# Softplus in two scans: from one activation to absolute value, exponential, logarithm and a sum

## The chip, the cores and the metric

The kernel runs on one core of one Trainium2 chip. The metric is the device time of one execution in microseconds (us). Three runs of the kernel before took 1286.11, 1288.93 and 1290.60 us; the median is 1288.93 us.

## The reference, cut to what matters

The reference is a stack of two layers over x of shape (1, 2048, 128), float32. Each part is added to x after a layer norm of its input:

```python
# layer 0, mixer: a state-space scan with 8 heads, 16 states
dt = softplus(zxbcdt[..., -NHEADS:] + dt_bias)          # (T, 8)
h  = exp(dt_t * A) * h + dt_t * x_t[..., None] * B_t    # A = -exp(A_log)
y  = sum(h * C_t) + D * x_t ; layer norm ; gate = sigmoid(y @ W_gate.T + b_gate)
# layer 0, ffn: causal attention (16 heads of 8), then 8 experts with exact gelu, top 2 gated
# layer 1, mixer: a scan with 256 channels and 16 states
xc    = silu(conv(x @ in_proj_w ...))
delta_s, B, u = split(xc @ x_proj_w + x_proj_b)
delta = softplus(delta_s @ dt_proj_w + dt_proj_b)       # (T, 256)
h     = exp(delta * A) * h + delta * B * u              # A = -1 ... -16
y     = (h.sum(-1) + u * D) * silu(z)
# layer 1, ffn: gated net with ternary weights, silu and gelu
```

The two uses of softplus are the subject: softplus(v) = log(1 + exp(v)), which equals max(v, 0) + log(1 + exp(-|v|)).

## The kernel before, in words

All engines run hand-written programs; every wait is a semaphore in `S`, and each engine works through its own list in order. Tokens are treated in NB = 4 blocks of BLK = 512, each of TPB = 4 chunks of 128.

**Mixer of layer 0.** Steps g = 0 ... 21, one per chunk (`chunk_act`, `chunk_front_dve` and so on), and between them pieces of the next block ("front", b+1) and of the last ("end", b-1), placed by `mixer_parts`: in step g with c = g % 4 the front part c of block g // 4 + 1 is done after the chunk's own work. `front_act` part 2 (L559 to L567) computes dt (Softplus, L563) and then two Silu into `sz` (L567); `front_late_dve` part 2 multiplies `sz` into `skip` (L713); in the next step `front_early_dve` part 3 makes dtA (L688) and its running sum cs (L694). `chunk_act` (L615) makes 8 exponentials of cs per chunk, `front_act` part 3 more exponentials (L574, L577) and four Silu (L581, L583). `end_act` part 3 is a Tanh (L641). At the very start ScalarE makes `a_neg` (L2424), and VectorE's first layer norm (L352) is queued behind the operation that reads it (L2452). The weights and the x of block 0 arrive under `in_x`.

**Attention** runs from about 200 to 720 us and is not touched. **Experts** (`moe_act`, `moe_pe`, `moe_dve`) go through 32 units k: ScalarE does Gelu on four tiles (L1630), TensorE the products up (L386 to L388) of unit k and down (L1620) of unit k-1, VectorE the gating (L1638). Block 0 of the second scan's front is put between the last units by `MF_PE`, `MF_ACT`, `MF_DVE`: dt products (L1896) and Softplus (L1963) at k = 29, u at 30 (L1884, L1948), du at 31 (L1998). The four banks of unit k's up product are freed one by one by unit k-1's Gelu.

**Scan of layer 1.** 64 steps (block b, state n). In each, ScalarE makes decay = exp(-(n+1) delta) of 128x1024 into psum (L2015) once step k-2 is scanned, and copies the last column of step k-2 (L2084); GpSimd makes drive = du * B of 128x1024 (L2055), up to five steps ahead; VectorE scans twice over 512 (L2077); TensorE adds the states up in psum (L2006). The front of block b+1 is spread over the 16 steps of block b by the tables `FRONT_PE`, `FRONT_ACT`, `FRONT_DVE`; an entry (n, part) is done on that engine after the work of step n:

```python
FRONT_PE  = [..., (8, "db"), (10, "dt"), (12, "u")]
FRONT_ACT = [..., (7, "xc"), (7, "gate"), (8, "db"), (11, "dt"), (12, "u")]
FRONT_DVE = [(-9, "stats"), (4, "conv0"), (5, "conv1"), (13, "du")]
```

"xc" and "gate" are Silu (L1939, L1942). "dt" on TensorE is L1896, on ScalarE the Softplus L1963 out of two psum banks. "u" on TensorE is L1884, whose two results go into the same two banks, so it waits for `c_dt_read`, which L1963 raises; on ScalarE "u" (L1948) waits for `c_u_filled`. "du" on VectorE is (u + bias) * delta (L1998); GpSimd's first drive of the next block waits for it (`delta_ready`). TensorE's own queue puts the sum of state k-3 ahead of the front parts of step k. The loads of ScalarE's function tables are not written in the source; the build puts one ahead of an activation whose function is not in the set that is loaded, and the profile shows it under that activation's line.

## Time and profile before

| | |
|---|---|
| median of 3 runs | 1288.93 us |
| the profiled execution | 1292.51 us, span 1290.7 us, mean granted clock 0.964 |
| PE (matmul) busy | 1147.6 us, 89% |
| VectorE (DVE) busy | 874.0 us, 68% |
| ScalarE (ACT) busy | 746.6 us, 58%, 1116 instructions |
| GpSimd (POOL) busy | 313.3 us, 24% |

The stages by the trace: layer 0 mixer 0 to about 200 us, attention to 720, experts to 946, scan to 1150, the last net to the end. Busy shares are means over stages that are bound by different engines, so each stage is read by itself. Times of rows are us from the span's start.

### The profile page before, as it was taken

What the parts mean: (1) busy time and instruction counts of PE and PEld (TensorE: products, weight loads), DVE (VectorE), ACT (ScalarE), POOL (GpSimd) and SP (SyncE); (2) the same over time, 40 slices, a digit from 0 to 9 for tenths busy, and PEclk for the clock granted to TensorE, in tenths of its full rate; (3) what the DMA queues carried; (4) which work ended last, traced back from release to release, by engine and by line L of the source; (5) the groups of instructions that cost most, each with busy time, mean ns of one, the idle gap of its engine ahead of it and who ended that gap; (6) DMA issues with size and microseconds to landing.
All of it is one profiled execution on the core that took longest, in us unless ns stands there. A gap on an engine that the chain in (4) does not pass through costs nothing.

```text
span 1290.7 us, 15518 instructions
## 1 busy us (share of the span) xinstructions
PE 1147.6 (89%) x5584; PEld 573.3 (44%) x5584; DVE 874.0 (68%) x1660; ACT 746.6 (58%) x1116; POOL 313.3 (24%) x260
## 2 busy tenths in 40 slices
PE   5799777888999999999999999999968889779998
PEld 2455443433333333333322565655523334347776
DVE  4788658958888888878843443444369999964443
ACT  5677532455665565646688544445658676435554
POOL 4323321210010000000011300000079788830000
PEclk9889889999999999989999999999989899889999
DMA  5210553344000000000000312211132223100000
GB/s 163 82 56 29 164 122 82 91 107 92 2 2 2 2 1 1 1 1 2 1 27 10 112 43 60 87 41 33 34 114 107 86 111 115 66 0 1 9 9 17
DMA packets 30491, 67.25 MB, mean 52 GB/s; under 512 B 3816, under 2 KB 16112, under 8 KB 28368
## 3 DMA queue, kind: packets, MB, share of 16 engines
q1 hardware_dynamic: 30416, 66.27, 17.7%
q8 instruction: 45, 0.74, 0.2%
q14 instruction: 30, 0.25, 0.1%
HBM read 57.47 MB, written 8.78 MB: 51 GB/s over the span
## 4 chain that ended last, share of the span: by engine, by line
PE 56%; DVE 15%; POOL 10%; issue 9%; ACT 9%; DMA 1%; SPq 0%; DVEq 0%; POOLq 0%; ACTq 0%
PE psum L1620 8%; PE psum L1328 8%; PE psum L1213 7%; PE psum L1282 6%; POOL drive L2055 6%; DVE mx L1225 6%; PE psum L386 5%; PE psum L388 5%; PE psum L387 5%; DVE hst L2077 2%; ACT probs L1296 2%; ACT psum L2015 1%; ACT edec L615 1%; PE psum L528 1%; PE psum L381 1%
## 5 line engine op out<-in xcount | busy, mean ns | idle before, releaser
L1225 DVE TENSOR_REDUCE mx<-psum 128x1 f32<-128x512 f32 (+3 forms) x640 | 349.2, 604 | 64.7 <-PE psum L1213 35.4
L1296 ACT ACTIVATE probs<-psum 128x1024 f32<-128x1024 f32 (+1 forms) x320 | 283.5, 936 | 171.7 <-PE psum L1282 151.3
L1213 PE MATMUL psum<-kz,qa 128*128 128x512 bf16 (+3 forms) x640 | 199.6, 354 | 22.6 <-DVE mx L1225 16.3
L1282 PE MATMUL psum<-qa,kz 128*128 128x512 bf16 (+1 forms) x640 | 174.9, 361 | 7.2 <-DMA qa<-m_rows 4.2
L1328 PE MATMUL psum<-probs,v 128*32 128x512 f32 (+3 forms) x1280 | 151.3, 544 | 1.5 <-POOL probs L1307 1.4
L1638 DVE TENSOR_TENSOR hid<-hid,gate_bc 128x1024 f32<-128x1024 f32 x64 | 79.0, 1241 | 106.7 <-ACT hid L1630 105.0
L2055 POOL TENSOR_TENSOR drive<-du,b_bc 128x1024 f32<-128x1024 f32 x64 | 148.7, 2359 | 1.4 <-issue 1.4
L2006 PE MATMUL psum<-hst,ident 128*128 128x512 f32 x256 | 122.1, 622 | 21.9 <-DVE u L2095 14.1
L1213 PEld LDWEIGHTS psum<-kz,qa 128*128 128x128 bf16 x640 | 57.1, 97 | 186.1 <-DVE mx L1225 136.9
L1630 ACT ACTIVATE hid<-psum,cols 128x512 f32<-128x512 f32 x128 | 84.7, 689 | 75.5 <-PE psum L388 75.3
L2077 DVE TENSOR_TENSOR_SCAN hst<-psum,hlast,drive 128x512 f32<-128x512 f32 x96 | 115.1, 1263 | 8.4 <-ACT psum L2015 6.4
L1307 POOL TENSOR_SCALAR_AFFINE_SELECT probs<-probs 128x512 f32<-128x512 f32 x48 | 29.4, 636 | 359.4 <-ACT probs L1296 359.4
L1620 PE MATMUL psum<-hid,ew_raw 128*128 128x512 f32 x256 | 115.4, 594 | 0.0
L2015 ACT ACTIVATE psum<-delta 128x1024 f32<-128x1024 f32 x64 | 65.6, 1025 | 55.4 <-DVE hst L2077 55.3
L2006 PEld LDWEIGHTS psum<-hst,ident 128*128 128x128 f32 x256 | 49.1, 198 | 89.8 <-issue 70.2
L1282 PEld LDWEIGHTS psum<-qa,kz 128*128 128x128 bf16 x640 | 57.3, 99 | 66.5 <-ACT probs L1296 26.9
L1620 PEld LDWEIGHTS psum<-hid,ew_raw 128*128 128x128 f32 x256 | 48.0, 189 | 51.5 <-issue 46.2
L652 DVE TENSOR_TENSOR fh_lo<-fh,fh_hi 128x512 fp32r<-128x512 f32 x48 | 32.1, 689 | 56.5 <-ACT fh_hi L2267 56.5
L386 PE MATMUL psum<-nx_hi,ew_lo 128*128 128x512 f32 x128 | 61.3, 479 | 1.0 <-POOL ew_lo L652 1.0
L386 PE MATMUL psum<-fh_hi,fw_lo 128*128 128x512 f32 x144 | 57.2, 398 | 5.4 <-DVE fh_lo L652 5.2
L388 PE MATMUL psum<-fh_hi,fw_hi 128*128 128x512 f32 x144 | 56.2, 390 | 0.0
L387 PE MATMUL psum<-fh_lo,fw_hi 128*128 128x512 f32 x144 | 56.1, 390 | 0.0
(285 smaller groups left out, 1687.8 us busy)
## 6 DMA issues: line engine op xcount, KB each, us to landing
b_bc<-b_rows SPq DMA_DIRECT2D x16, 1024.0 KB, 4.7
cs_bc<-cs_rows SPq DMA_DIRECT2D x16, 512.0 KB, 4.7
gate_bc<-gate_rows SPq DMA_DIRECT2D x32, 256.0 KB, 3.2
qk_part_rows<-qk_parts SPq DMA_DIRECT2D x48, 128.0 KB, 2.3
ew_raw<-experts_dram SPq DMA_DIRECT2D x8, 512.0 KB, 3.6
qa<-qk_part_rows SPq DMA_DIRECT2D x16, 192.0 KB, 5.3
kz<-qk_part_rows SPq DMA_DIRECT2D x16, 192.0 KB, 5.9
fw_raw<-net_dram SPq DMA_DIRECT2D x11, 256.0 KB, 2.7
```

Of the source, the lines that this page charges most:

```text
L386: pe.matmul(out, w[1], x[0], start=start, stop=False, skip_group_check=True)
L387: pe.matmul(out, w[0], x[1], start=False, stop=False, skip_group_check=True)
L388: return pe.matmul(out, w[0], x[0], start=False, stop=stop, skip_group_check=True)
L1213: ins = pe.matmul(out[:, 0:w], qa[:, b, h // 2, i * P:(i + 1) * P], key_rows(h, c)[:, 0:w], start=True, stop=not last, skip_group_check=True)
L1225: dve.tensor_reduce(mx[:, 4 * i + h % 4, c:c + 1], fill_bank("mx", k, n)[:, 0:w], AX.X, ALU.max).then_inc(S["mx_read"], 1)
L1282: ins = pe.matmul(out[:, lo:], key_rows(h, kt // TPB)[:, kt % TPB * P:(kt % TPB + 1) * P], qa[:, b, h // 2, lo:], start=True, stop=not dia ...
L1296: act.activation(probs[:, st % 2, hh, :, lo:], s_pair[n % 2][:, :, lo:], ACT.Exp, scale=SCALE).then_inc(S["p_done"], 1)
L1328: ins = pe.matmul(out[32 * hh:32 * hh + 32, own:], v9[:, at:at + 32], probs[:, st % 2, hh, j, own:], start=(kt == 0), stop=(kt == TPB * (b ...
L1620: ins = pe.matmul(bank[b][:, :], ew_raw[e % EW_SLOTS][:, FC + m, :], hid[:, n % HID_SLOTS, m, :], start=False, stop=(n == block_end[b] and ...
L2006: ins = pe.matmul(bank[j][:, :], ident[:, :], hst[:, (NS1 * b + n) % HBUF, j, :], start=(n == 0), stop=(n == NS1 - 1))
L2055: pool.tensor_tensor(drive[:, k % DRIVE_SLOTS, :, :], du[:, b % 2, :, :], rows.unsqueeze(1).broadcast_to([P, 2, BLK]), ALU.mult).then_inc( ...
L2077: ins = dve.tensor_tensor_scan(hst[:, k % HBUF, j, :], decay[k % 2][:, j, :], drive[:, k % DRIVE_SLOTS, j, :], init, ALU.mult, ALU.add)
```

## The change

Both Softplus are replaced. In the mixer, part 2 makes |v| into a new tile `dta`, max(v, 0) into dt, exp(-|v|) and log(1 + .) in `dta`, and VectorE adds the two ahead of dtA. In the second scan ScalarE makes |v| from both banks into delta, then one exponential and one logarithm over 128x1024; VectorE adds max(v, 0) from psum in a new part "dsum" at step 12 and raises `c_dt_read`. "u" moves from step 12 to 13 on TensorE and ScalarE, "du" from 13 to 14; in the experts "dsum" is at k = 30 and "u" at 31. The bias of the second softplus moves into the product: row 32 of its weights, against a row of `dB` that is 1. A table set that holds exponential and logarithm is loaded by name: once at the start, in chunks with g % 4 of 0 or 3, and after "gate". Semaphores of the gate loads and of the cs loads become one set, with counts to match. The diff, cut:

```diff
+        EXP_LN = "natural_log_exp_and_others"
 # front_act, part 2
-                act.activation(dt[b % 2][:, :], pj(DTREP), ACT.Softplus, bias=C("dt_bias")).then_inc(S["pj_act"], 1)
+                if b >= 1:
+                    act.wait_ge(S["dt_done"], b)
+                o.did(act.activation(dta[:, :], pj(DTREP), ACT.Abs, bias=C("dt_bias")))
+                act.activation(dt[b % 2][:, :], pj(DTREP), ACT.Relu, bias=C("dt_bias"))
+                o.wait()
+                o.did(act.activation(dta[:, :], dta[:, :], ACT.Exp, scale=-1.0))
+                o.wait()
+                act.activation(dta[:, :], dta[:, :], ACT.Ln, bias=one[:, 0:1]).then_inc(S["pj_act"], 1)
 # chunk_act, after its waits
+            if g % TPB in (0, TPB - 1):
+                act.preload_act_table_set(EXP_LN)
 # front_early_dve, part 3
                 dve.wait_ge(S["pj_act"], 5 * b + 3)
+                o.did(dve.tensor_tensor(dt[b % 2][:, :], dt[b % 2][:, :], dta[:, :], ALU.add))
+                o.wait()
 # experts
-        MF_PE = {..., 29: ("dt",), 30: ("u",)}
+        MF_PE = {..., 29: ("dt",), 31: ("u",)}
-                  29: ("dt",), 30: ("u",)}
-        MF_DVE = {21: ("stats",), 26: ("conv0",), 27: ("conv1",), 31: ("du",)}
+                  29: ("dt",), 31: ("u",)}
+        MF_DVE = {21: ("stats",), 26: ("conv0",), 27: ("conv1",), 30: ("dsum",), 31: ("du",)}
-        gate_in = [S[f"gate_in{n}"] for n in range(G_SLOTS)]
+        gate_in = cs_in
-            dve.wait_ge(gate_in[n % G_SLOTS], 16 * (n // G_SLOTS + 1))
+            dve.wait_ge(gate_in[n % G_SLOTS], 16 * len(range(n % G_SLOTS, G, CS_SLOTS)) + 16 * (n // G_SLOTS + 1))
 # tables of the scan (FRONT_PE; RING_FRONT changes as it does)
-        FRONT_PE = [..., (10, "dt"), (12, "u")]
-        FRONT_ACT = [..., (11, "dt"), (12, "u")]
-        FRONT_DVE = [(-9, "stats"), (4, "conv0"), (5, "conv1"), (13, "du")]
+        FRONT_PE = [..., (10, "dt"), (13, "u")]
+        FRONT_ACT = [..., (11, "dt"), (13, "u")]
+        FRONT_DVE = [(-9, "stats"), (4, "conv0"), (5, "conv1"), (12, "dsum"), (14, "du")]
 # scan_front_act, "gate"
                 act.activation(sz1[b % 2][:, :, :], sz1[b % 2][:, :, :], ACT.Silu).then_inc(S["sz_ready"], 1)
+                act.preload_act_table_set(EXP_LN)
 # scan_front_act, "dt"
                 for m in range(2):
                     act.wait_ge(S["c_dt_filled"], 2 * b + m + 1)
-                    act.activation(delta[:, b % 2, m, :], scan_bank("dt", b, m)[:, :], ACT.Softplus,
-                                   bias=C("dt1_b", m)).then_inc(S["c_dt_read"], 1)
+                    o.did(act.activation(delta[:, b % 2, m, :], scan_bank("dt", b, m)[:, :], ACT.Abs))
+                o.wait()
+                o.did(act.activation(delta[:, b % 2, :, :], delta[:, b % 2, :, :], ACT.Exp, scale=-1.0))
+                o.wait()
+                act.activation(delta[:, b % 2, :, :], delta[:, b % 2, :, :], ACT.Ln, bias=one[:, 0:1]).then_inc(S["c_ln_done"], 1)
 # scan_front_dve
+            elif part == "dsum":
+                dve.wait_ge(S["c_ln_done"], b + 1)
+                for m in range(2):
+                    dve.scalar_tensor_tensor(delta[:, b % 2, m, :], scan_bank("dt", b, m)[:, :], 0.0, delta[:, b % 2, m, :],
+                                             ALU.max, ALU.add).then_inc(S["c_dt_read"], 1)
 # ScalarE's program
             act.wait_ge(S["in_x"], 32)
+            act.preload_act_table_set(EXP_LN)
 # host_layout
+    dtw[2 * NS1] = x["L1_attn_dt_proj_b"]
-    pad = np.zeros(P - 2 * NS1, np.float32)
+    pad = np.eye(1, P - 2 * NS1, dtype=np.float32)[0]
```

## Rows read from the trace of the kernel before

**Rows 1.** The page, the chain that ended last, share of the span by engine

```profile
PE 56%; DVE 15%; POOL 10%; issue 9%; ACT 9%; DMA 1%; SPq 0%; DVEq 0%; POOLq 0%; ACTq 0%
```

**Rows 2.** Stages, 968 to 1017: us, busy of PE, PEld, DVE, ACT, POOL, clock, DMA

```profile
968.00:1017.00 49.00, 40.09 (x94) 16.56 (x92) 45.91 (x53) 35.80 (x60) 42.92 (x24) 1.00 0.30 103
```

**Rows 3.** VectorE's scans (L2077): what they waited for, us and times

```profile
  ACT psum L2015: 15.6, 9
```

**Rows 4.** Groups of ScalarE, shapes apart: count, busy us, mean ns, idle before

```profile
L1963 ACT ACTIVATE delta<-psum,cols 128x512 f32<-128x512 f32 x8 | 5.2, 685 | 2.9 <-PE psum L1896 2.9
...
L1963 ACT ACT_TABLE_LOAD x4 | 5.1, 1283 | 0.1
...
L558 ACT ACTIVATE convin<-psum 128x512 f32<-128x512 f32 x8 | 4.8, 598 | 6.6 <-PE psum L447 6.6
...
L1942 ACT ACTIVATE sz_odd<-sz_odd 128x1024 f32<-128x1024 f32 x2 | 2.1, 1056 | 0.0
```

**Rows 5.** In order of time, the start: start us, us, engine, line, what, idle

```profile
0.78 1.28 ACT L2423 ACT_TABLE_LOAD   x1 [0.78 <-PEq L2597]
3.76 0.20 ACT L2423 ACTIVATE half_gate<-cols 128x2 f32<-128x2 f32 x1 [1.69 <-DMA cols<-cols_dram]
```

**Rows 6.** VectorE at the start, in order of time

```profile
4.28 0.87 DVE L352 BATCH_NORM_STATS2 ln_st<-x_tok 128x6 f32<-128x128 f32 x4
```

**Rows 7.** ScalarE in the mixer, in order of time, block 1

```profile
47.47 1.28 ACT L563 ACT_TABLE_LOAD   x1
...
50.77 1.09 ACT L567 ACTIVATE sz<-psum 128x512 f32<-128x512 f32 x2
```

**Rows 8.** VectorE in the mixer, in order of time, blocks 1 to 3

```profile
51.49 1.28 DVE L713 TENSOR_TENSOR skip<-psum,sz 128x512 f32<-128x512 f32 x2
...
64.52 0.15 DVE L739 COPY dt_tok<-psum 128x8 f32<-128x8 f32 x1
...
86.07 1.29 DVE L713 TENSOR_TENSOR skip<-psum,sz 128x512 f32<-128x512 f32 x2 [1.99 <-ACT sz L567]
...
122.01 1.29 DVE L713 TENSOR_TENSOR skip<-psum,sz 128x512 f32<-128x512 f32 x2 [0.99 <-ACT sz L567]
```

**Rows 9.** ScalarE in the last chunk of the mixer, in order of time

```profile
166.43 2.44 ACT L615 ACTIVATE edec<-cs_bc,ncs_tok 128x128 f32<-128x128 f32 x8 [2.41 <-issue]
169.04 0.69 ACT L641 ACTIVATE sg<-psum,half_gate 128x512 f32<-128x512 f32 x1 [0.17 <-PE psum L520]
```

**Rows 10.** ScalarE in the experts: the Gelu of unit 30, in order of time

```profile
922.40 2.42 ACT L1630 ACTIVATE hid<-psum,cols 128x512 f32<-128x512 f32 x4
```

**Rows 11.** TensorE in the experts and the scan, in order of time

```profile
926.36 3.60 PE L1884 MATMUL psum<-xc,sw 128*128 128x512 f32 x8
...
981.56 3.70 PE L1884 MATMUL psum<-xc,sw 128*128 128x512 f32 x8 [1.02 <-ACT delta L1963]
```

**Rows 12.** ScalarE in the scan, steps 11 to 13 of block 0

```profile
979.52 1.28 ACT L1963 ACT_TABLE_LOAD   x1
...
983.39 1.03 ACT L2015 ACTIVATE psum<-delta 128x1024 f32<-128x1024 f32 x1
...
985.30 0.69 ACT L1948 ACTIVATE u<-psum,cols 128x512 f32<-128x512 f32 x1 [0.18 <-PE psum L1884]
```

**Rows 13.** VectorE in the scan, steps 12 to 15 of block 0

```profile
984.46 4.82 DVE L2077 TENSOR_TENSOR_SCAN hst<-psum,drive 128x512 f32<-128x512 f32 x4 [1.68 <-ACT psum L2015]
989.19 1.38 DVE L1998 SCALAR_TENSOR_TENSOR du<-psum,cols,delta 128x512 f32<-128x512 f32 x2
990.49 2.33 DVE L2077 TENSOR_TENSOR_SCAN hst<-psum,drive 128x512 f32<-128x512 f32 x2
```

**Rows 14.** GpSimd in the scan: the first drives of block 1

```profile
990.71 13.91 POOL L2055 TENSOR_TENSOR drive<-du,b_bc 128x1024 f32<-128x1024 f32 x6 [0.71 <-issue]
```

**Rows 15.** TensorE in the scan, after its two waits of 3.24 us

```profile
1004.74 8.82 PE L2006 MATMUL psum<-hst,ident 128*128 128x512 f32 x20 [3.24 <-DVE u L2095]
...
1056.89 10.52 PE L2006 MATMUL psum<-hst,ident 128*128 128x512 f32 x20 [3.24 <-DVE u L2095]
```

More of the change, by code:

```diff
@@ L51 @@
     ("fc1_b", NE * FC), ("in1_b", 4), ("conv1_w", 2 * CONV), ("conv1_b", 2), ("xu_b", 2), ("xdB_b", 1),
-    ("dt1_b", 2), ("d1", 2), ("w1_s", HC), ("w2_s", HC), ("h1_s", HC), ("h2_s", HC), ("w3_s", 1),
+    ("d1", 2), ("w1_s", HC), ("w2_s", HC), ("h1_s", HC), ("h2_s", HC), ("w3_s", 1),
     ("out1_b", 1),
@@ L164, in build @@
         convin = sb("convin", [P, 2, CONV - 1 + BLK], F32)
+        dta = sb("dta", [P, BLK], F32)
         free[0] = max(free[0], KZ[1][1])
@@ L334, in build @@
             bo_added mx_read mrow_done on_done back_copied att_done mx_filled mneg_done mrow_filled p_done p_causal
-            s_scores pv_done o_copied tok_filled back_filled att_filled rden_done gate_in0 nx2_split lg_done
-            gT_done gelu_done moe_added nx2_ready lg_filled gates_done gT_filled lgm_done ex8_done ew_split
-            gate_in1 hid_filled slot_in2 down_done hid_gated slot_in3 ew_split_hi gate_in2 moe_copied
+            s_scores pv_done o_copied tok_filled back_filled att_filled rden_done nx2_split lg_done
+            c_ln_done gT_done gelu_done moe_added nx2_ready lg_filled gates_done gT_filled lgm_done ex8_done ew_split
+            hid_filled slot_in2 down_done hid_gated slot_in3 ew_split_hi moe_copied
             moe_turned moe_pool_consts in_moe c_in_read c_u_read c_db_read c_dt_read b_saved c_mixed
@@ L585, in build @@
         cs_rows = nc.dram_tensor("cs_rows", (NB, TPB, H0, P), F32, kind="Internal").ap()
-        cs_in = [sem(f"cs_in{n}") for n in range(CS_SLOTS)]
+        cs_in = [sem(f"ring_in{n}") for n in range(CS_SLOTS)]
         def cs_save_sp(sp, b):
@@ L1810, in build @@
         LN_C = 3 * NB
-        FRONT_PE = [(0, "turn"), (1, "x"), (2, "z"), (8, "db"), (10, "dt"), (12, "u")]
-        FRONT_ACT = [(-1, "apply"), (0, "hi"), (2, "x"), (3, "z"), (3, "tap"), (7, "xc"), (7, "gate"), (8, "db"), (11, "dt"), (12, "u")]
-        FRONT_DVE = [(-9, "stats"), (4, "conv0"), (5, "conv1"), (13, "du")]
+        FRONT_PE = [(0, "turn"), (1, "x"), (2, "z"), (8, "db"), (10, "dt"), (13, "u")]
+        FRONT_ACT = [(-1, "apply"), (0, "hi"), (2, "x"), (3, "z"), (3, "tap"), (7, "xc"), (7, "gate"), (8, "db"), (11, "dt"), (13, "u")]
+        FRONT_DVE = [(-9, "stats"), (4, "conv0"), (5, "conv1"), (12, "dsum"), (14, "du")]
         FRONT_POOL = [(-2, "ln")]
-        RING_FRONT = [(0, "turn"), (1, "x"), (2, "z"), (3, "tap"), (8, "db"), (10, "dt"), (12, "u")]
+        RING_FRONT = [(0, "turn"), (1, "x"), (2, "z"), (3, "tap"), (8, "db"), (10, "dt"), (13, "u")]
         EARLIEST = -9
@@ L2581, in host_layout @@
         "xu_b": vec(xpb[2 * NS1:], 2), "xdB_b": vec(np.concatenate([xpb[0:2 * NS1], pad]), 1),
-        "dt1_b": vec(x["L1_attn_dt_proj_b"], 2),
         "d1": vec(x["L1_attn_D"], 2), "w1_s": vec(x["L1_ffn_w1_s"], HC), "w2_s": vec(x["L1_ffn_w2_s"], HC),
```

2 lines of the change are left out of this document (1 added, 1 removed).

## The prediction

> **What bounds the kernel now.** I began with the page's chain [rows 1]: it is mixed, so no single engine's saving can be read off as time, and the change has to be followed stage by stage. It touches three places: the mixer of layer 0 (0 to 200 us), the last units of the experts, and the scan. The table by stage for one block of the scan [rows 2] shows VectorE busy 45.9 of 49.0 us and GpSimd 42.9, ScalarE only 35.8. So the scan is VectorE's, with ScalarE of interest where VectorE waits for a decay: 15.6 us in nine waits over the whole scan [rows 3]. The timelines then give each place of the change.
>
> **Loads of tables.** A load takes 1.28 us [rows 4]. The load ahead of each Softplus goes (four at L563, four at L1963), and in the scan's three fronts the reload ahead of the next decay: 11. To come: one in the experts after "gate", two in the experts' dt (below), one at g = 15, where a set with the exponential is in already, and one for the Tanh behind it: 5. Six fewer in all; the other named loads stand where a load stood.
>
> **The start, +1.3.** Now the first load runs at 0.78, ahead of the wait for `cols`, and costs nothing [rows 5]. By name it stands behind the wait: `half_gate` starts 1.28 later, then `a_neg`, and VectorE's first layer norm, which starts at 4.28 right behind it [rows 6], moves by as much. Nothing covers it: all later work hangs on this norm. Bounds 0 (if the build hoists it) and 1.3; I take 1.3, since an engine's list is in order.
>
> **The mixer's four blocks, +3.5.** ScalarE: out go a load and 0.69. In come Abs and Relu (0.69 like L563, the second overlapping by 0.1), an exponential (0.60, the Copy of 128x512 in [rows 4]) and a logarithm with a bias column (0.69), with two waits for itself of some 0.05: 2.7 for 1.97, so +0.7 [rows 4, 7]. Trace and page do not differ here. VectorE: one sum of 128x512, half of `skip`'s pair, 0.65 to 0.7 [rows 8], ahead of dtA. Block 0: `sz` comes while VectorE does its convolution, the sum is open: 0.7. Block 1: `sz` ends at 51.86 and `skip` starts at 51.49 as it comes [rows 7, 8]; from there VectorE has no idle time to 64.5, so both count: 1.4. Blocks 2 and 3: VectorE waits 1.99 and 0.99 for `sz` [rows 8], so ScalarE's 0.7 counts, and the sum lies beside TensorE's gate products, on whose Tanh VectorE waits next: 0.7 each, 1.4 each without that cover. Sum 3.5, bounds 2 and 6.
>
> **Chunk 15, +1.3.** Its exponentials run from 166.43 to 168.87, and Tanh starts at 169.04 [rows 9]. A redundant load ahead of them and one ahead of Tanh put Tanh at 171.4, 2.4 later; its second half was held by TensorE to 170.76, so VectorE's product after it moves by 1.3. 
>
> **The experts, +1.3.** At k = 29 Softplus gives way to two Abs (0.60 each), an exponential of 128x1024 (1.06 [rows 4]) and a logarithm (1.15, that plus the 0.09 by which L1963 exceeds L558): 3.4 for 1.3. The set of Gelu is in and none is named there, so I count a load for the exponential and one for the logarithm, both behind the input; the load of Softplus ran while ScalarE waited for its input and cost nothing. The Gelu of unit 30, from 922.40 now [rows 10], thus starts 2.1 + 2 * 1.28 = 4.7 later, at 927.1, and frees its first bank at 927.8. TensorE now goes on at 926.5 with "u" [rows 11]; after the change the up product of unit 31 comes there and wants this bank: 1.3 idle. The load after "gate" is hidden, as the Gelu behind it ends 3 us before TensorE needs it. Bounds 0 and 3. The dsum at k = 30 has 2 us to spare before "u".
> A rule against my count: the Trainium skill, "ScalarE activation tables: per-element evaluation and per-set limits", section "Table sets in the compiler and the runtime", has loads placed by the greedy longest run, which would serve Abs, Exp and Ln with one load; the 1.3 would then be about 0. No row of before has a run that two sets could serve, so the trace is silent; it is a rival below.
>
> **The scan, three fronts, +3.35 each.** At step 11 ScalarE now spends 979.52 to 983.39 on load, Softplus, load [rows 12]: 3.87. After: 0.50 + 0.60 + 1.06 + 1.15 and two waits, 3.35. So step 12, which waits 1.68 for its decay [rows 13], starts 0.55 earlier. This is all that the six loads give here, since what replaces them is nearly as long.
> Then it is lost. TensorE's "u" needs the two banks, and only VectorE's dsum frees them, after step 12. Count from the end E of step 12. Now: step 13 (2.3), du (1.3), steps 14 and 15: step 14 starts at E + 3.6 [rows 13]. After: the first half of dsum to E + 0.74 (du's form, 1.38 for two [rows 13]), then "u" on TensorE 3.70 [rows 11], ScalarE's second read 0.69, and behind that read in ScalarE's list decay 14, 1.03 [rows 12]: step 14 starts at E + 6.2. Behind the waiting read stand decay 14 and everything later on ScalarE; VectorE has only the rest of dsum and step 13 meanwhile (to E + 3.6) and idles 2.6. Then du (1.3) follows step 14 where it went before it. So 6.2 + 1.3 - 3.6 = 3.9, less 0.55: 3.35, three times: 10.05.
> GpSimd's first drive of the next block (2.32) goes 0.14 behind du [rows 14]. Now two steps (4.5) lie between du and the step that needs this drive; after, one (2.3): late by 0.2 at most, taken as nothing.
> TensorE's clock: before "u" it now idles 1.02 [rows 11], afterwards some 4.7. Of two waits of 3.24 one left 20 products at 8.82 us, the other at 10.52 [rows 15]: between 0 and 1.7 each. I take 0.5, as a fall may also come after the products: 1.5. Scan +11.5; bounds 2 and 16.
>
> **Sum.** 1.3 + 3.5 + 1.3 + 1.3 + 11.5 = 18.9 on the profiled execution's 1292.5 (span 1290.7 and 1.8 around it): 1311.4. The median of the runs is 3.6 lower: 1307.8, say 1308. Attention and the last net are unchanged. A run-to-run difference of 0.3% (3.9 us) is about what the measurement can tell.
>
> **Rivals.**
> (1) As forecast: 1308, own range 1302 to 1315. Chance 0.60.
> (2) One load fewer in the experts (the rule above): 1308 - 1.3 = 1306.7. Chance 0.12, as nothing in the trace speaks.
> (3) The late "u" is covered. If ScalarE's read of u did not hold decay 14, each front would cost dsum's 1.3 less 0.55: 2.3 in all and no clock loss: 1298.7. Against it: the order of ScalarE's list. Chance 0.10.
> (4) Faster. The mechanism is the loads in front of the decays: in each front VectorE idles for the decay around step 12 (1.68 in block 0 [rows 13]) and after "gate", 15.6 in nine waits [rows 3]. If dsum fell into such idle time and all six loads lay on the path, 6 * 1.28 = 7.7 would come off: 1281. It decides where decay 12 comes at least 1.3 earlier than now; by my count it comes 0.55 earlier, as the new activations fill the place. Chance 0.07.
> (5) The change does not do what it says: a set loaded by name is not kept by the build's placement, and each Exp and each Ln brings its own load: in the scan 2 * 1.28 more per front, in the mixer 1.28 per block: + 7.7 + 5.1: 1321. Chance 0.06.
> (6) Gains and losses cancel, within 0.3%: "u" covered and most of the mixer's terms too. Chance 0.05.
>
> **How the numbers follow.** The time is that of (1). Range 1297 to 1316: it holds (1) with its bounds, (2) and (3), and leaves out (4), (5), (6), 0.18. Faster: (4), 0.07. Within 0.3%: (6), 0.05. Slower: the rest, 0.88.
>
> **What would show it.** Right: six fewer table loads, none at L563 or at the scan's "dt"; the first norm at about 5.6; in the experts Gelu of unit 30 near 927 + 6; per front of the scan, VectorE idle 2 to 3 us after step 13 for a decay, TensorE's "u" 3 us later than now and behind dsum, ScalarE waiting for u. Scan 10 to 13 us longer. Wrong: step 14 starting right behind step 13, decays 12 coming more than 1 us earlier, or the mixer's end moved by less than 2 us.

## The result, and the profile after

The changed kernel takes 1320.49 us (median of 4 runs, 1319.09 to 1322.39), against 1288.78 us before: ratio 1.0249, interval 1.0226 to 1.0271, so 32 us slower. The direction was forecast and the size was not: the forecast was 1308 us, with a range of 1297 to 1316. The profiled execution took 1320.8 us, span 1319.0, mean granted clock 0.954.

The page, the chain of work that ended last, which answers to [rows 1]:

```profile
PE 10%; POOL 3%; DVE 1%; ACT 1%; issue 1%; DVEq 0%; POOLq 0%; ACTq 0%
```

The shares don't sum to 100 here: this chain could be followed back only a short way, so it can't be compared with [rows 1] and I read stages instead. Groups of ScalarE, shapes apart (count, busy us, mean ns, idle before), beside [rows 4]:

```profile
L625 ACT ACT_TABLE_LOAD x8 | 10.3, 1283 | 12.1 <-issue 8.3 <-DVE ncs_tok L754 3.8
...
L1982 ACT ACTIVATE delta<-delta,one 128x1024 f32<-128x1024 f32 x4 | 4.6, 1148 | 0.1
L1978 ACT ACTIVATE delta<-psum 128x512 f32<-128x512 f32 x8 | 4.4, 586 | 4.3 <-PE psum L1910 4.3
L1980 ACT ACTIVATE delta<-delta 128x1024 f32<-128x1024 f32 x4 | 4.2, 1058 | 0.1
...
L653 ACT ACT_TABLE_LOAD x1 | 1.3, 1283 | 0.0
...
L1980 ACT ACT_TABLE_LOAD x1 | 1.3, 1283 | 0.0
L1982 ACT ACT_TABLE_LOAD x1 | 1.3, 1283 | 0.0
```

The durations are those of the forecast (1.15 for the logarithm, 1.06 for the exponential of 128x1024), and so is the list of loads: 43 instead of 49, one more for Tanh at L653, one each for the experts' exponential and logarithm, none at the scan's "dt". The start, ScalarE in order of time, beside [rows 5]:

```profile
4.01 1.28 ACT L2446 ACT_TABLE_LOAD   x1 [4.01 <-DMA cols<-cols_dram]
5.31 0.20 ACT L2447 ACTIVATE half_gate<-cols 128x2 f32<-128x2 f32 x1
...
17.11 0.69 ACT L568 ACTIVATE dta<-psum,cols 128x512 f32<-128x512 f32 x1 [1.11 <-PE psum L448]
...
20.96 1.08 ACT L577 ACTIVATE sz<-psum 128x512 f32<-128x512 f32 x2
```

`half_gate` is 1.55 later. In block 0 `sz` is 3.3 later (20.96 against 17.65), so ScalarE loses 1.75 in this block, where 0.7 was counted. Before, ScalarE there read as follows:

```profile
13.73 0.60 ACT L558 ACTIVATE convin<-psum 128x512 f32<-128x512 f32 x1 [0.93 <-PE psum L447]
14.35 1.28 ACT L563 ACT_TABLE_LOAD   x1
15.65 0.69 ACT L563 ACTIVATE dt_even<-psum,cols 128x512 f32<-128x512 f32 x1
```

The Softplus load ran from 14.35 to 15.63, and its input came at about 15.6 (17.11 after, less the 1.55). It was hidden behind TensorE, and taking it out gave nothing. In block 3 ScalarE came to "dt" late, in block 2 the load ran behind the wait for the input (0.68), and both paid it in full; block 1 paid most of it (by my estimate, from ScalarE's wait of 0.43 for the input there in after). So in block 0 `sz` comes too late for VectorE, which before had no wait here:

```profile
21.66 1.29 DVE L727 TENSOR_TENSOR skip<-psum,sz 128x512 f32<-128x512 f32 x2 [2.06 <-ACT sz L577]
```

It starts 2.6 later than before (19.08), 1.0 more than the start gives, and the sum behind it adds 0.7.

The scan, VectorE in order of time around step 12 of block 0, beside [rows 13]:

```profile
1001.29 2.34 DVE L2100 TENSOR_TENSOR_SCAN hst<-psum,drive 128x512 f32<-128x512 f32 x2 [0.92 <-ACT psum L2038]
1003.55 1.26 DVE L2013 SCALAR_TENSOR_TENSOR delta<-psum,delta 128x512 f32<-128x512 f32 x2
1004.73 2.33 DVE L2100 TENSOR_TENSOR_SCAN hst<-psum,drive 128x512 f32<-128x512 f32 x2
1011.18 2.34 DVE L2100 TENSOR_TENSOR_SCAN hst<-psum,drive 128x512 f32<-128x512 f32 x2 [4.13 <-ACT psum L2038]
1013.43 1.38 DVE L2021 SCALAR_TENSOR_TENSOR du<-psum,cols,delta 128x512 f32<-128x512 f32 x2
```

Why it idles is in ScalarE's list:

```profile
1007.83 0.69 ACT L1963 ACTIVATE u<-psum,cols 128x512 f32<-128x512 f32 x1 [5.40 <-PE psum L1898]
1009.54 0.69 ACT L1963 ACTIVATE u<-psum,cols 128x512 f32<-128x512 f32 x1 [1.03 <-PE psum L1898]
1010.13 1.02 ACT L2038 ACTIVATE psum<-delta 128x1024 f32<-128x1024 f32 x1
```

and in TensorE's, beside [rows 11]:

```profile
1004.27 5.24 PE L1898 MATMUL psum<-xc,sw 128*128 128x512 f32 x8 [4.08 <-DVE delta L2013]
```

This is the mechanism forecast: dsum frees the banks, "u" follows, ScalarE waits for it, decay 14 stands behind. But VectorE idles 4.13 us (3.99 and 3.87 in the other two fronts) instead of 2.6, since "u" itself takes 5.24 us where [rows 11] have 3.70.

**Where the 32 us lie.** Single profiles of the same code differ by some us in a stage, so I read each stage also in those experiments (below) whose code is the same there. Times in us: the start of the first Gelu (where the experts begin), of the load at which the scan begins, and of the load at which the last net begins; "scan" is the difference of the last two, and the last column is TensorE's mean granted clock over the first 250 us.

| kernel | first Gelu | scan's load | net's load | scan | clock 0 to 250 |
|---|---|---|---|---|---|
| before | 720.1 | 946.9 | 1151.8 | 204.9 | 0.92 |
| after | 735.9 | 964.4 | 1180.4 | 216.0 | 0.87 |
| mixer_of_before | 717.8 | 946.2 | 1162.4 | 216.2 | 0.92 |
| scan_of_before | 734.1 | 961.8 | 1164.6 | 202.8 | 0.88 |
| u_read_late | 732.2 | 960.6 | 1169.9 | 209.3 | 0.90 |
| loads_hidden | 726.4 | 954.8 | 1173.4 | 218.6 | 0.89 |
| before_start_load | 724.2 | 951.0 | 1151.8 | 200.8 | 0.90 |
| mixer_no_sum | 724.0 | 952.4 | 1176.2 | 223.8 | 0.92 |
| mixer_block0 | 723.6 | 952.0 | 1168.0 | 216.0 | 0.92 |
| unguarded | 719.4 | 946.1 | 1147.5 | 201.4 | 0.92 |
| all_mended | 734.2 | 961.0 | 1168.4 | 207.4 | 0.86 |
| before_filled | 716.2 | 944.0 | 1146.8 | 202.8 | 0.98 |
| after_filled | 724.5 | 954.1 | 1172.3 | 218.2 | 0.97 |
| all_mended_filled | 721.2 | 948.0 | 1158.1 | 210.1 | 0.97 |
| unguarded_filled | 715.4 | 942.2 | 1143.6 | 201.4 | 0.99 |

To the first Gelu the changed mixer takes 734.1 (median of after, scan_of_before and u_read_late), that of before 719.0 (before and mixer_of_before): 15.1. The experts add 1.7. The scan takes 217.2 as changed (median of six) and 202.8 as before (four profiles): 14.4. The sum is 31.2, against 31.7 by the medians of the runs. The forecast had 6.1, 1.3 and 11.5.

### The profile page after: what moved, and what is told of

The parts are those of the page before. It is cut to its first block and busy times, and to the rows that moved or that the text cites. A ratio compares the mean times of both kernels' runs of the same rounds, so it can differ in the third digit from the quotient of the medians.

```text
span 1319.0 us, 15547 instructions
## 1 busy us (share of the span) xinstructions
PE 1160.5 (88%) x5584; PEld 581.0 (44%) x5584; DVE 881.7 (67%) x1672; ACT 752.6 (57%) x1130; POOL 313.0 (24%) x260
## 5 line engine op out<-in xcount | busy, mean ns | idle before, releaser
L1227 PE MATMUL psum<-kz,qa 128*128 128x512 bf16 (+3 forms) x640 | 200.8, 356 | 22.5 <-DVE mx L1239 16.3
L2029 PE MATMUL psum<-hst,ident 128*128 128x512 f32 x256 | 121.6, 620 | 19.9 <-DVE u L2118 14.4
L2100 DVE TENSOR_TENSOR_SCAN hst<-psum,hlast,drive 128x512 f32<-128x512 f32 x96 | 115.4, 1262 | 15.1 <-ACT psum L2038 11.4
L1230 PE MATMUL psum<-identb,maskneg 128*128 128x128 bf16 x256 | 56.4, 224 | 0.0
```

The costliest lines, as they stand in the source:

```text
L1227: ins = pe.matmul(out[:, 0:w], qa[:, b, h // 2, i * P:(i + 1) * P], key_rows(h, c)[:, 0:w], start=True, stop=not last, skip_group_check=True)
L2029: ins = pe.matmul(bank[j][:, :], ident[:, :], hst[:, (NS1 * b + n) % HBUF, j, :], start=(n == 0), stop=(n == NS1 - 1))
L2100: ins = dve.tensor_tensor_scan(hst[:, k % HBUF, j, :], decay[k % 2][:, j, :], drive[:, k % DRIVE_SLOTS, j, :], init, ALU.mult, ALU.add)
```

## The experiments

The ratio is to the kernel before, run on the same chip beside it (its median there was 1290.4 to 1291.3 us). The changed kernel's 1.0249 is from its own comparison, in which the kernel before took 1288.8, and carries 0.0022 (3 us) to either side. So "less than the changed kernel" is given twice: by the ratios, and in brackets by the medians in us, which give 1 to 3 us less. Either is good to about 4 us.

**u_read_late.** The read of u one step later on ScalarE:

```diff
-        FRONT_ACT = [... (11, "dt"), (13, "u")]
+        FRONT_ACT = [... (11, "dt"), (14, "u")]
```

> The changed kernel, with ScalarE's read of u moved one step later (step 14 instead of 13 in each of the scan's three fronts), so that decay 14 stands ahead of the read in ScalarE's list. Nothing of the computation is changed. Theory of the forecast (the read of u, held by the banks that only dsum frees, holds decay 14 and so VectorE for 2.6 us in each front): the 2.6 us go three times, about 7.8 us less than the changed kernel (some 1312.7 us, ratio to before 1.0185), and VectorE shows no wait of over 1 us for a decay at step 14. Rival (the scan's loss is something else: TensorE's clock, or the first drive on GpSimd, late behind du): less than 2 us less than the changed kernel.

1309.61 us, 1.0146 (1.0114 to 1.0178). VectorE in order of time, the same place:

```profile
999.83 1.26 DVE L2013 SCALAR_TENSOR_TENSOR delta<-psum,delta 128x512 f32<-128x512 f32 x2
1001.00 4.55 DVE L2100 TENSOR_TENSOR_SCAN hst<-psum,drive 128x512 f32<-128x512 f32 x4
1005.48 0.72 DVE L2021 SCALAR_TENSOR_TENSOR du<-psum,cols,delta 128x512 f32<-128x512 f32 x1
1006.57 0.75 DVE L2021 SCALAR_TENSOR_TENSOR du<-psum,cols,delta 128x512 f32<-128x512 f32 x1 [0.37 <-ACT u L1963]
1008.00 2.34 DVE L2100 TENSOR_TENSOR_SCAN hst<-psum,drive 128x512 f32<-128x512 f32 x2 [0.69 <-ACT psum L2038]
1010.88 2.46 DVE L2100 TENSOR_TENSOR_SCAN hst<-psum,hlast,drive 128x512 f32<-128x512 f32 x2 [0.54 <-POOL drive L2078]
```

Steps 13 and 14 now run as one piece (4.55), so the order of ScalarE's list was the cause, and the scan is 7.9 us shorter (209.3 against 217.2), as forecast. The time fell by more, 13 us (11); the rest lies ahead of the scan, where this kernel has the changed kernel's code (first Gelu 732.2 against 735.9). What remains over the scan of before, 6.5 us, is in these rows and the one of step 12 (997.57 us, a wait of 0.92 as in after): step 12 gains 0.76 (0.92 for 1.68); dsum adds 1.2, du's wait 0.4, the wait of step 15 for its decay 0.7, the first drive late on GpSimd 0.5. That is 2.0 a front, 6.1 for three.

**mixer_of_before.** The changed kernel with the mixer's edits undone:

```diff
-                o.did(act.activation(dta[:, :], pj(DTREP), ACT.Abs, bias=C("dt_bias")))
-                act.activation(dt[b % 2][:, :], pj(DTREP), ACT.Relu, bias=C("dt_bias"))
...
+                act.activation(dt[b % 2][:, :], pj(DTREP), ACT.Softplus, bias=C("dt_bias")).then_inc(S["pj_act"], 1)
...
-                act.preload_act_table_set(EXP_LN)
...
-                o.did(dve.tensor_tensor(dt[b % 2][:, :], dt[b % 2][:, :], dta[:, :], ALU.add))
```

> The changed kernel with the mixer of layer 0 as before (Softplus on ScalarE, no sum on VectorE, no loads by name in the start and in the mixer); experts and scan stay as changed. Nothing of the result is changed. Theory A (the mixer's terms are worth what the landmarks of the two traces show, 15.8 us, because each small delay is paid again further on, among others in a lower granted clock of TensorE): 15 to 16 us less than the changed kernel, 1304 to 1305.5 us, ratio to before 1.012 to 1.013. Rival B (the mixer is worth its linear sum of 6.1 us, and the rest of the shift at 720 us is something the runs vary in): 6 us less, about 1314 us, ratio 1.020.

1305.26 us, 1.0110 (1.0073 to 1.0146): 18 us less than the changed kernel (15). Rival B is out; theory A's 1.012 to 1.013 lies in the interval. The mixer and the start are worth 15 to 18 us.

**scan_of_before.** The changed kernel with the edits of the experts' last units and of the scan undone (Softplus, "u" at 12, "du" at 13, no dsum, no load behind "gate").

> The changed kernel with the experts' last units and the scan as before (Softplus on ScalarE, u at step 12, du at 13, no dsum, no load by name behind gate); the mixer stays as changed. Nothing of the result is changed. Theory A (landmarks: mixer 15.8, experts 1.7, scan 11.1): 12.8 us less than the changed kernel, about 1307.5, ratio to before 1.0145. Rival B (mixer 6.1 only): the scan then carries the rest, 1298, ratio 1.007. A and B together with the run of the mixer of before have to add up to the whole difference of 31.7 us.

1303.97 us, 1.0096 (1.0066 to 1.0127): 20 us less (16.5). Theory A as expected (1.0145) missed. Its 12.8 us came from two profiles alone, and the one of before had a long scan (204.9; the other three with this code 200.8 to 202.8); with the medians of the table the experts and the scan are worth 1.7 + 14.4 = 16.1. Rival B's 1.007 lies in the interval, but mixer_of_before excludes that rival. By ratios the two undoings add up to 38 us where the whole is 32, by medians to 31.7, so no overlap of the two is shown.

**loads_hidden.** Two groups of loads by name:

```diff
-            act.wait_ge(S["in_x"], 32)
             act.preload_act_table_set(EXP_LN)
+            act.wait_ge(S["in_x"], 32)
...
-            if g % TPB in (0, TPB - 1):
+            if g % TPB in (0, TPB - 1) and g < 3 * TPB:
```

> The changed kernel with two groups of loads by name changed and nothing else: the one of the start stands ahead of the wait for the constants, and the two of chunks 12 and 15 of the mixer's last block are left out (those of blocks 0 to 2 stay). Nothing of the result is changed. By the linear sum: 1.3 to 1.55 for the start and 1.3 for chunk 15, 2.6 to 3 us less than the changed kernel, about 1317.5, ratio to before 1.022. By the theory that a delay in the mixer is paid again in TensorE's granted clock: 5 to 8 us less, 1312 to 1315. The traces are compared by the time of the first Gelu's load (734.6 in the changed kernel, 718.8 before) and by TensorE's granted clock to 250 us.

1315.83 us, 1.0193 (1.0156 to 1.0229): 7 us less (5), for 2.6 to 3 us of loads. The interval holds the linear sum's 1.022 as well as the 5 to 8 us less of the clock's theory, so this run doesn't decide between them. First Gelu 726.4.

**before_start_load.** The kernel before with a load behind the wait:

```diff
             act.wait_ge(S["in_x"], 32)
+            act.preload_act_table_set("exp_and_others")
```

> The kernel before, with one thing added: a load by name, of the set with the exponential, behind ScalarE's wait for the constants, so that everything starts 1.3 to 1.55 us later and nothing else is different. Nothing of the computation is changed. Linear theory: 1.3 to 1.55 us over before at every later landmark and at the end, ratio 1.0010 to 1.0012. Theory of the clock (a delay in the first 60 us shifts TensorE's stretches at 1.2 GHz onto its long products, and is paid again): 3 to 6 us over before by the last exponential of the mixer (166.4 in before) and at the end, ratio 1.0023 to 1.005, with more than 41 us at the half clock before 240 us.

1291.44 us (12 runs), 1.0009 (0.9993 to 1.0026): near the linear theory; of the clock's 1.0023 to 1.005 only the low end lies in the interval. The single profile shows the other picture at first: `sz` of block 0 1.6 later, the last exponentials of the mixer 5.4 later, granted clock to 250 us 0.90 instead of 0.92; then the scan is 4 us shorter than in before's profile, and both reach the net's load at 1151.8. So this small delay was not paid several times over in the median, though up to the first Gelu its one profile looks as if it were (724.2 against 720.1). That TensorE's slow stretches fall differently from run to run, and that the median evens this out, would explain both; it isn't shown.

**mixer_no_sum.** VectorE's `dt + dta` left out.

> The changed kernel without VectorE's sum in the mixer's four blocks: dt is then max(x, 0) alone in layer 0, which is a change of the computation; all of ScalarE's work, its loads and the rest are as changed. Forecast's terms: the sum is worth 0.7 (block 0) and 0.7 (block 1), hidden in blocks 2 and 3: 1.4 us less than the changed kernel, ratio 1.0238. If it lies on the path in all four blocks: 2.8, ratio 1.0227. If a delay is paid again in the clock: 5 us or more less, ratio below 1.021.

1314.94 us, 1.0189 (1.0165 to 1.0213): 8 us less (5.6) for four sums of 0.68 each (2.7 us busy). Both 1.0238 (the forecast's 1.4 us) and 1.0227 (all four sums on the path) lie outside the interval. By the landmarks the sum is worth 1.8 us at `sz` of block 3 (127.40 for 129.19) and 5.0 at the exponentials of chunk 12 (147.00 for 151.98). The 3.2 between lie at the place below, where the clock fell in after and not here.

**mixer_block0.** Blocks 1 to 3 as before, block 0 and the start as changed.

> The changed kernel with blocks 1 to 3 of the mixer as before (Softplus, no sum, no loads by name); the start and block 0 stay as changed. Nothing of the result is changed. Theory A (the mixer's excess is made in the start and block 0, where the load of Softplus used to lie hidden behind TensorE's input, and where a granted clock of 1.2 GHz falls on the first transition between blocks): the last exponential of the mixer comes 7 us or more later than in before (166.4), and the end is 5 to 6 us below the changed kernel, ratio 1.020 to 1.021. Rival B (the excess is made in blocks 1 to 3, block by block): the last exponential 3.3 to 4.8 us later than in before, and the end 8 to 11 us below the changed kernel, ratio 1.0165 to 1.0185.

1311.55 us, 1.0171 (1.0143 to 1.0198): 10 us less (9), which is rival B: the excess is made in blocks 1 to 3, where the linear sum with chunk 15 sees 4.1 us. The last exponentials come only 2.0 later than in before (168.41 against 166.43), less than either expectation had, although the start alone gives 1.5. The clock to 250 us is 0.92, as in before.

**Where the excess sits.** TensorE around the end of block 2, after:

```profile
128.02 0.63 PE L512 MATMUL psum<-ident,yn 128*128 128x128 f32 x4 [0.82 <-ACT dta L573]
129.84 0.83 PE L512 MATMUL psum<-ident,yn 128*128 128x128 f32 x4 [1.19 <-ACT sz L577]
...
135.27 4.89 PE L455 MATMUL psum<-x0T,wk 128*128 128x512 f32 x9
```

and before:

```profile
120.11 0.63 PE L511 MATMUL psum<-ident,yn 128*128 128x128 f32 x4 [0.38 <-ACT dt_odd L563]
121.93 0.66 PE L511 MATMUL psum<-ident,yn 128*128 128x128 f32 x4 [1.19 <-ACT sz L567]
125.03 7.03 PE L454 MATMUL psum<-x0T,wk 128*128 128x512 f32 x16
```

The bank that "yn" goes to is freed by ScalarE's "dt" and `sz`, so the longer run of activations makes TensorE wait 0.82 instead of 0.38. Stretches of before and after, with the granted clock in the third column from the end:

```profile
120.00:136.00 16.00, 14.19 (x61) 7.34 (x61) 12.82 (x34) 13.92 (x26) 5.53 (x5) 1.00 0.31 100
```
```profile
128.00:145.00 17.00, 15.79 (x58) 8.98 (x59) 11.79 (x33) 12.97 (x25) 5.66 (x5) 0.80 0.29 95
```

The clock is 1.00 in the one and 0.80 in the other, and the products take 0.54 us each (4.89 / 9) instead of 0.44 (7.03 / 16). From here the shift grows from 7.9 to 11.1 us.

The longer wait is not enough to bring the slow stretch. Eight profiles have a wait of 0.81 or 0.82 here, with the same 1.19 behind it, and only four of them are slow at this place (after, u_read_late, scan_of_before and all_mended, granted clock 0.80 to 0.90). The other four (loads_hidden, mixer_no_sum, and after_filled and all_mended_filled below) show 1.00, as do the seven with 0.38 or no wait. TensorE in after_filled, which has nothing added at this place:

```profile
124.81 0.63 PE L518 MATMUL psum<-ident,yn 128*128 128x128 f32 x4 [0.82 <-ACT dta L579]
...
129.73 7.03 PE L460 MATMUL psum<-x0T,wk 128*128 128x512 f32 x16
```

So what came earlier decides too, and how isn't shown. A second such place is chunk 4: TensorE waits 2.70 for its decays before and 4.71 after, which is followed by transposes at 0.42 instead of 0.27 us, and the shift grows from 6.6 to 7.1. After, then before:

```profile
70.21 0.48 PE L468 MATMUL psum<-ident,dt_odd 128*128 128x128 f32 x1 [4.71 <-POOL cdec_odd L741]
70.48 0.42 PE L469 MATMUL psum<-ident,cs_odd 128*128 128x128 f32 x1
```
```profile
63.80 0.33 PE L467 MATMUL psum<-ident,dt_odd 128*128 128x128 f32 x1 [2.70 <-POOL cdec_odd L727]
63.97 0.27 PE L468 MATMUL psum<-ident,cs_odd 128*128 128x128 f32 x1
```

At a third the wait did not grow at all. TensorE idles 5.92 us ahead of the second norm in both kernels, but in after it stays slow for longer behind it, and the shift grows from 3.3 to 4.8. After, then before:

```profile
46.22 2.89 PE L448 MATMUL psum<-x0T,w_raw 128*128 128x512 f32 x4
```
```profile
41.92 1.88 PE L447 MATMUL psum<-x0T,w_raw 128*128 128x512 f32 x4
```

These places only suggest a cause. To test it I filled TensorE's idle time with products that nobody uses, and kept every wait (the edit adds one, ahead of the first v).

**after_filled and before_filled.** The same edit in the changed kernel and in the one before:

```diff
+        def busy(pe, out, n):
+            for i in range(TPB * n):
+                pe.matmul(out[:, i % TPB * P:(i % TPB + 1) * P], ident[:, :], ident[:, :], start=True, stop=True)
+
         def ln_pe(pe, u, out):
+            busy(pe, out, {1: 8, NB: 3, NB + 1: 3}.get(u, 0))
             pe.wait_ge(S["ln_xn"], u + 1)
...
-            pe.wait_ge(S["dec_done"], b + 1)
             if g >= 1:
                 pe.wait_ge(S["tok_dve"], 4 * g - 1)
+            busy(pe, turn_a, {0: 7, 4: 4}.get(g, 0))
+            pe.wait_ge(S["dec_done"], b + 1)
...
             elif part == "v":
+                if b == 0:
+                    pe.wait_ge(S["tok_dve"], 4 * 14 - 1)
+                    busy(pe, turn_a, 8)
                 out = prep_take(pe, "pv", b)
```

> The changed kernel with TensorE kept at work in six places of the mixer where it waits for other engines anyway: small products (ident by ident, 128x128, 20 us in all at 2.4 GHz) into a bank that it already holds, overwritten right after. Nothing of the result is changed. The places are the waits for the decays of chunks 0 and 4, for the second layer norm, for the two norms of attention's preparation, and the one ahead of its first v. Theory (the mixer's excess over its linear sum is time at 1.2 GHz, which TensorE's idle stretches bring): half-clock time before 240 us falls from 65 us (51 to 65 in three profiles of the same mixer) to under 30, the start of the first Gelu from 732 to 736 to below 727, and the end is 6 to 12 us under the changed kernel, ratio to before 1.015 to 1.020. Rival (the clock is not what the delay comes from, the waits for VectorE and ScalarE are): less than 2 us gained, or lost where a product lies in the way, ratio 1.023 or more.

> The kernel before with the same products in the same six waits of TensorE. Nothing of the result is changed. Theory: before has 41 us at half clock before 240 us and loses some of them too: 3 to 8 us faster than before, ratio 0.994 to 0.998; and the difference to the changed kernel with the same products is then the linear sum of the change: about 7 (start and mixer) + 2 (experts) + 11 (scan) = 20 us, not 32. Rival (the fillers gain nothing, or lie in the way): 0.999 or more.

after_filled 1313.15 us, 1.0182 (1.0161 to 1.0202); before_filled 1287.39 us, 0.9974 (0.9956 to 0.9992). Both came out as the theory had it. The first 250 us of the changed kernel, and of the same with the products:

```profile
0.00:250.00 250.00, 192.42 (x969) 110.10 (x969) 170.37 (x478) 133.08 (x272) 70.46 (x85) 0.87 0.36 96
```
```profile
0.00:250.00 250.00, 211.94 (x1301) 131.44 (x1301) 181.50 (x508) 138.81 (x280) 73.71 (x87) 0.97 0.37 97
```

TensorE is busy for 20 us more in sum, and in the same time VectorE gets through 30 instructions more (the fourth column). TensorE in order of time, at the waits for chunk 0 and the second norm:

```profile
27.63 6.41 PE L381 MATMUL psum<-ident 128*128 128x128 f32 x56
...
34.93 7.41 PE L381 MATMUL psum<-ident 128*128 128x128 f32 x64
42.18 0.60 PE L387 MATMUL psum<-ident,xn 128*128 128x128 f32 x4
```

The four transposes of `xn` take 0.60 here and 1.08 in after. The products came out too long: each is two instructions in the trace (64 for 32, at 0.116 us), and in the six places they take 30.5 us where 20 were expected. At the first wait TensorE is late by that: the first exponentials come 2.2 us later in before_filled than in before, 0.9 later in after_filled than in after, of which 0.4 was there before the wait in each. The net gains of 3.4 us (3.0) and 8.6 us (7.3) are after this cost.

The pair gives what was wanted: with the clock held near its upper level, the change costs 5.3 us at the third `nx` of attention's preparation (233.06 against 227.74) where it cost 15.7 in the first two profiles (245.09 against 229.37), and 8.3 instead of 15.1 at the first Gelu. Each of these is one profile against one, and 0.75 of the 5.3 and 8.3 is there from the start, where `cols` came late in after_filled (`half_gate` at 6.32 against 4.02). By medians the whole change costs 25.8 us instead of 31.7. From the spread of the runs that difference of 5.9 is good to about 4 us, so it is clear of zero, but not well measured. The expectation of 20 us for the whole missed, in the main because the scan costs 14 to 15 and not 11.

**all_mended.** The start's load and the loads from chunk 12 on as in loads_hidden, u read at 14, and

```diff
+                if b == 0:
+                    act.preload_act_table_set(EXP_LN)
                 for m in range(2):
                     act.wait_ge(S["c_dt_filled"], 2 * b + m + 1)
```

> The changed kernel with four mendings together: the start's load ahead of the wait, no loads by name from chunk 12 on, one load of the set of both functions ahead of the experts' dt (in place of one for the exponential and one for the logarithm), and the read of u at step 14. Nothing of the result is changed. The two runs of parts gave 0.0103 (u) and 0.0056 (loads) of before's time over the changed kernel's 1.0249; the experts' load should give 1.3 us: 1.007 to 1.009 of before. If the parts were not additive, since the clock's stretches differ from run to run: 1.004 to 1.013. In the experts one load stands ahead of Abs, Exp and Ln, and the Gelu of unit 30 comes 1.3 us sooner after dt.

1308.42 us, 1.0137 (1.0117 to 1.0157): out of the additive range, and above the wider one (1.004 to 1.013) too. By medians the shortfall is smaller: 12.1 us gained, where the parts promised 10.9 + 4.7 + 1.3 = 16.9, which is about what the noise allows. ScalarE in order of time shows that the experts' mending did what it should:

```profile
929.55 1.28 ACT L1977 ACT_TABLE_LOAD   x1
933.57 0.60 ACT L1980 ACTIVATE delta<-psum 128x512 f32<-128x512 f32 x1 [2.74 <-PE psum L1910]
...
935.06 1.06 ACT L1982 ACTIVATE delta<-delta 128x1024 f32<-128x1024 f32 x1
936.15 1.15 ACT L1984 ACTIVATE delta<-delta,one 128x1024 f32<-128x1024 f32 x1
```

One load, hidden ahead of the input, serves all, and the scan begins 45.5 us after the load ahead of "xc" (L1953), as in before (L1939; 47.2 in after). The scan takes 207.4. The lack is in the mixer: its code is that of loads_hidden, yet the first Gelu starts at 734.2 and not at 726.4, with a clock of 0.86 instead of 0.89. So two profiles of the same code can differ by 8 us at this point.

**all_mended_filled and unguarded_filled.** Whether the parts add once the clock is held.

> The changed kernel with the four mendings (start's load ahead of the wait, no loads by name from chunk 12 on, one load for the experts' dt, u read at step 14) and with TensorE kept at work in the six waits of the mixer. Nothing of the result is changed. Theory (parts add where TensorE's clock in the mixer is held): from the changed kernel with the same products (1.0182) the u of the scan takes 7 to 10 us, the start and chunk 15 take 2.6, the experts 1.3 to 1.7: 1.006 to 1.010. Rival (the four mendings were worth only 1.0249 less 1.0137 for another reason than the clock): 1.012 or more. First Gelu's start below 722 by the theory, near 725 by the rival.

> The kernel without the guard (logarithm of 1 plus exponential, both on ScalarE; the guard for large arguments is the part left out) with TensorE kept at work in the six waits of the mixer. Alone the one gave 0.9981 of before and the other 0.9974. Theory: they add, 0.995 to 0.996. Rival (both took the same half-clock time away, so they don't add): 0.9975 to 0.9985.

all_mended_filled 1298.47 us, 1.0062 (1.0039 to 1.0085), first Gelu 721.2: the theory, in both numbers. With the idle time filled the mendings take 0.0120 off (1.0182 less 1.0062), 15 us, of a forecast of 0.008 to 0.012; without, they took 0.0112 off, where the separate runs had promised 0.017. The two are nearly the same, so the pair doesn't show that it was the clock that kept all_mended from its sum. The first Gelu does bear out the 8.3 above: it comes 5.0 later than in before_filled (721.2 against 716.2), about 8.3 less the 3 us of the two mended loads.

unguarded_filled 1286.73 us, 0.9964 (0.9947 to 0.9981), granted clock 0.99 to 250 us: the point lies between theory and rival and the interval holds both, so additivity isn't settled there. It is below both kernels; the guard is left out.

**unguarded.** Exponential and logarithm on ScalarE with no Abs, Relu, Max or sum:

```diff
-                    act.activation(delta[:, b % 2, m, :], scan_bank("dt", b, m)[:, :], ACT.Softplus,
-                                   bias=C("dt1_b", m)).then_inc(S["c_dt_read"], 1)
+                    act.activation(delta[:, b % 2, m, :], scan_bank("dt", b, m)[:, :], ACT.Exp).then_inc(S["c_dt_read"], 1)
+                act.wait_ge(S["c_dt_read"], 2 * b + 2)
+                act.activation(delta[:, b % 2, :, :], delta[:, b % 2, :, :], ACT.Ln, bias=one[:, 0:1]).then_inc(S["c_ln_done"], 1)
```

> Softplus in both scans as the logarithm of 1 plus the exponential, both on ScalarE, without the guard for large arguments, which is the part of the computation that is left out; no sums on VectorE, all steps of the scan where they were before (u at 12, du at 13), the start's load ahead of the wait, no loads by name from chunk 12 on, one load of the set of both functions ahead of the experts' dt. Per front of the scan ScalarE spends 2 exponentials of 128x512 and one logarithm of 128x1024, about 2.4 us, where before it spent 3.87 on load, Softplus, load. Theory: VectorE's wait for decay 12 (1.68 us in block 0 of before) goes nearly in full: 1.5 us less three times, and the mixer costs 0.1 to 0.7 per block more than Softplus did plus the hidden load of block 0 that is no longer needed: 2 to 5 us below before, 0.996 to 0.9985. Rival (VectorE's wait only moves, to the wait behind it on GpSimd's drives): same as before, 0.999 to 1.001. If a change of the mixer by itself costs clock, it comes out slower than before, over 1.003.

1287.73 us (12 runs), 0.9981 (0.9966 to 0.9996), as the theory had it, though the rival's 0.999 lies in the interval too. VectorE in block 0:

```profile
979.72 4.54 DVE L2088 TENSOR_TENSOR_SCAN hst<-psum,drive 128x512 f32<-128x512 f32 x4
984.90 2.34 DVE L2088 TENSOR_TENSOR_SCAN hst<-psum,drive 128x512 f32<-128x512 f32 x2 [0.65 <-ACT psum L2026]
```

and ScalarE:

```profile
983.26 0.69 ACT L1956 ACTIVATE u<-psum,cols 128x512 f32<-128x512 f32 x1 [0.74 <-PE psum L1891]
```

Steps 11 and 12 are one piece (4.54), so the 1.68 for decay 12 is gone in full. The 0.65 stands ahead of step 13: its decay waits in ScalarE's list behind the read of u, the same order that costs the changed kernel its 4.13. In the other two fronts 1.44 for decay 12 goes and 1.22 and 1.23 for decay 13 come (0.29 and none before), so the three fronts gain 1.0, 0.5 and 0.2, and the scan is 1.4 shorter (201.4 against 202.8).

The run shows what saving the loads is worth when only an exponential and a logarithm take Softplus's place: 0.2%. Of the kernels that compute all of it, before_filled is the fastest, 0.9974, faster than the kernel before and the changed one.

## Why the prediction was wrong

Right, by its own steps: the direction; the list of loads, place by place; the durations; the start (1.55 for 1.3); chunk 15 (the shift grows from 11.1 at chunk 14's exponentials to 12.9 at the `nx` behind Tanh, in loads_hidden from 7.2 to 7.5, so the loads cost 1.5 for 1.3; the Tanh brings its own, L653); the experts (1.7 for 1.3), where rival (2), one load for three functions, fell: L1980 and L1982 each bring one. This is against what I had drawn from the greedy longest run of the Trainium skill, "ScalarE activation tables: per-element evaluation and per-set limits", section "Table sets in the compiler and the runtime"; here Exp and Ln stood side by side with a set for both at hand, and the build loaded twice. In the scan the mechanism was right, in each link.

Wrong, three steps:

**TensorE's clock: 1.5 us in the scan, and nothing at all in the mixer.** This is the step that failed. I priced the clock in the scan alone, and summed the mixer (3.5) as if TensorE ran on at a fixed rate. Before the first Gelu 15.1 us came instead of 6.1. before_filled and after_filled put 7 of these 15 us (15.1 less 8.3) down to the clock, and by the medians 6 of the whole 32, give or take 4. The trace of before could have warned of it: the granted clock was 0.92 to 250 us, which by my estimate is some 40 us at the lower of the two levels (twice 8% of 250). The Trainium skill, "TensorE: Matmul & The Clock Gate", section "Part 1: The HAM clock gate", has the array fall to 1.2 GHz after idle time and come back after work; the rows above agree (4.71 idle, then transposes at 0.42 us for 0.27). What they don't show is what decides at the shorter waits, where a wait of 0.82 was followed by a slow stretch in four profiles of eight.

**The mixer's block 0, 0.7.** The forecast had ScalarE lose 0.7, covered by VectorE's convolution, and only the sum (0.7) count. The load taken out was part of that reckoning as a gain, but it was hidden, as [rows 7] of block 1 could not tell. So ScalarE lost 1.75, VectorE had to wait for `sz`, and the block cost 1.0 + 0.7 = 1.75. (That is the profile of after. From `half_gate` to `sz` the profiles with the changed block 0 take 14.9 to 15.7 us, those with the old one 13.7 to 14.0.) Blocks 1 to 3 by the same two profiles: `sz` of block 1 +1.0 and the sum +0.9 (1.4 forecast), blocks 2 and 3 +0.4 each (0.7 each forecast). That makes 4.4 without the slow stretches, for 3.5 forecast with bounds of 2 and 6.

**The scan, 3.70 for "u" on TensorE.** It takes 5.24 us, behind 4.08 of idle time; the stretch from 1003 to 1012 has a granted clock of 0.81. Step 14 starts 7.55 behind the end E of step 12, and not 6.2. So a front costs 7.55 + 1.3 (du) - 3.6 (before) - 0.76 (step 12 comes earlier) = 4.5, and 0.3 ahead of the next block's first step: 4.8, three times 14.4, where 3.35 + 0.5 was forecast. The comparison of the scans gives 14.4 too. The clock's cost was thought of as a tail of the accumulating products and not as a longer "u" in the very chain that VectorE waits for.

Put together: 8.3 (start, mixer, chunk 15 with the clock held), 6.8 (the clock there), 1.7 (experts) and 14.4 (scan) make 31 of the 31.7. Of the 8.3, 5.3 are there at 233 us, within the 6.1 forecast for this part; the other 3 come up in attention, and why stays open. The rivals: (3) would have needed the read of u behind decay 14, and u_read_late shows that place as worth 7.9 us; (4) is excluded, as decay 12 came 0.76 earlier and the fronts still lost; (5) is excluded by the count of loads, and (6) by the 32 us.

## What to carry to other kernels

Before taking a table load out, look for what ended the wait of the activation behind it: a load that runs while the input is still on its way is free, and what replaces it is not. Where a stage shows a granted clock well under 1, don't forecast it by the linear sum alone: here such a stage cost 15.1 us, and 8.3 with the clock held. Widen the range upwards, for the products behind TensorE's waits above all where others wait for them, or give TensorE something to do in the wait; a rule for each microsecond isn't shown. And in a list in program order, a read that waits for a late result belongs behind the work that others need soon: moving one by a step was worth 8 us here.
